# Moving the bias products and phi of a linear-attention stage off TensorE and VectorE

## What is computed

```python
x = x + 0.5 * ffn(layernorm(x))
x = x + attn(layernorm(x))
x = x + 0.5 * ffn(layernorm(x))

def attn(x):
    q = phi(split_heads(x @ Wq.T + bq))      # phi(z) = elu(z) + 1 = max(z, 0) + exp(min(z, 0))
    k = phi(split_heads(x @ Wk.T + bk))
    v = split_heads(x @ Wv.T + bv)
    kv_prefix = cumsum(k[..., :, None] * v[..., None, :], axis=rows)
    k_prefix = cumsum(k, axis=rows)
    out = (q . kv_prefix) / (q . k_prefix + 1e-6)
    return merge_heads(out) @ Wo.T + bo
```

## Time and profile before

| | |
|---|---|
| median of 3 runs | 388.18 us (387.33 to 390.04) |
| the profiled execution, own time | 387.34 us |
| its span in the profile | 385.6 us |
| PE, PEld busy | 312.6, 247.8 us |
| DVE, ACT, POOL busy | 228.4, 133.3, 241.6 us |
| mean granted TensorE clock | 0.91 |

### The profile page before, as it was taken

One profiled execution on the slowest core, in us unless ns is written; L12 is line 12 of the kernel. 1 busy time (PEld: TensorE's weight loads), 2 busy tenths in 40 slices (PEclk: granted clock), 3 DMA queues, 4 the chain that ended last, 5 costly groups with the idle time before them and its releaser, 6 DMA issues. The chain is left out here.

```text
span 385.6 us, 8340 instructions
## 1 busy us (share of the span) xinstructions
PE 312.6 (81%) x1964; PEld 247.8 (64%) x1970; DVE 228.4 (59%) x590; ACT 133.3 (35%) x375; POOL 241.6 (63%) x317
## 2 busy tenths in 40 slices
PE   2855699888888993899999999576798889989940
PEld 1832498887787871366677776333798788878820
DVE  5889364344333445979888889688244434333437
ACT  2205243332332335233455553333343223332322
POOL 5047567777777763564655556527677777777744
PEclk9997689999999997589999999655899999999995
DMA  7440466665555617000000000002476555555347
GB/s 210 139 122 2 109 153 192 159 164 163 135 155 162 164 48 218 2 0 0 15 14 14 12 9 20 24 7 60 126 194 166 154 159 152 152 155 156 111 146 202
DMA packets 35362, 41.88 MB, mean 109 GB/s; under 512 B 4808, under 2 KB 21840, under 8 KB 35344
## 3 DMA queue, kind: packets, MB, share of 16 engines
q1 hardware_dynamic: 30352, 31.44, 30.3%
q0 software_dynamic: 4992, 10.23, 8.8%
HBM read 33.39 MB, written 8.26 MB: 108 GB/s over the span
## 5 line engine op out<-in xcount | busy, mean ns | idle before, releaser
L401 POOL DMA_INDIRECT xg<-xn_rows,src_row x78 | 75.9, 973 | 33.3 <-issue 22.6
L408 POOL DMA_INDIRECT y_rows<-y_tile,dst_row x78 | 76.9, 985 | 24.0 <-issue 22.3
L1023 PE MATMUL banks<-xgT,w1b 128*128 128x128 f32 x624 | 89.1, 288 | 2.0 <-DMA w1b<-in_W1b 1.2
L768 DVE TENSOR_TENSOR h_pre<-banks,w1b 128x512 f32<-128x512 f32 x78 | 53.9, 691 | 58.4 <-PE banks L1023 57.0
L1032 PE MATMUL banks<-w,h_act 128*128 x624 | 87.1, 283 | 0.2
L1023 PEld LDWEIGHTS banks<-xgT,w1b 128*128 128x128 f32 x624 | 78.8, 198 | 4.9 <-DMA w1b<-in_W1b 1.4
L1032 PEld LDWEIGHTS banks<-w,h_act 128*128 128x128 f32 x624 | 75.5, 191 | 4.5 <-issue 0.8
L516 ACT COPY xgT<-banks 128x128 f32<-128x128 f32 x78 | 20.7, 265 | 125.7 <-PE banks L1042 125.7
L778 DVE COPY y_tile<-banks 128x128 f32<-128x128 f32 x78 | 22.7, 291 | 61.4 <-DMA y_rows<-y_tile,dst_row 55.5
L523 ACT ACTIVATE h_act<-h_pre 128x512 f32<-128x512 f32 x78 | 49.3, 632 | 5.8 <-DVE h_pre L768 5.8
L439 POOL TENSOR_TENSOR kv<-qk,vx 128x1024 f32<-128x1024 f32 x16 | 31.5, 1968 | 27.7 <-DVE qk L808 27.7
(11 more groups left out here) (182 smaller groups left out, 433.3 us busy)
## 6 DMA issues: line engine op xcount, KB each, us to landing
w1b<-in_W1b SPq DMA_DIRECT2D x78, 258.0 KB
y_back<-y_rows SPq DMA_DIRECT2D x16, 256.0 KB, 5.0
xg<-xn_rows,src_row POOLq DMA_INDIRECT x78
y_rows<-y_tile,dst_row POOLq DMA_INDIRECT x78
x<-in_L_attn_x SPq DMA_DIRECT2D x4, 256.0 KB, 3.8
xn_rows<-xn SPq DMA_DIRECT2D x4, 256.0 KB, 3.0
xn_rows<-xn_ring SPq DMA_DIRECT2D x16, 64.0 KB, 1.5
out<-x SPq DMA_DIRECT2D x4, 256.0 KB, 2.6
```

Source lines behind the costliest of these rows:

```text
L401: g.indirect_dma_start(out=xg[:, n % RING, :], out_offset=None, in_=xn_rows[f][:, :], in_offset=bass.IndirectOffsetOnAxis(ap=src_row[:, n: ...
L408: g.indirect_dma_start(out=y_rows[f][:, :], out_offset=bass.IndirectOffsetOnAxis(ap=dst_row[:, i:i + 1], axis=0), in_=y_tile[:, i % RING, ...
L768: v.tensor_tensor(h_pre[:, r, :].rearrange("p (c n) -> p c n", c=FC), h_bank(r).rearrange("p (c n) -> p c n", c=FC), w1b[:, r, DF:DF + FC] ...
L1023: last = mm(h_bank(q)[:, c * P:(c + 1) * P], w1b[:, q, c * P:(c + 1) * P], xgT[:, q, :], start=True, stop=True)
```

## The change

The attention's layer norm multiplies by `rstd` and adds `shift`. The new kernel adds 1 to the shift, so that each normed row sums to 128; it centres the weights (subtracts the mean over the input features) and adds bias / 128 to each of their rows. Three products on PE build this `w_fold` once. The host hands over the four weights turned and side by side, and the four biases as one row. The output bias is added to x by POOL for two tiles at a time (`add_bo`), and DVE's residual waits for it. The positive part of phi is a new ACT operation, `relu`, and the sum with `expo` is a new POOL operation at the head of `outer`.

```diff
@@ constants, loads
+            sp.dma_start(w_attn[:, :], Wa).then_inc(attn_in, 16)
+            sp.dma_start(bias[:, :], ba).then_inc(attn_in, 16)
             for t in range(NT):
                 sp.dma_start(b2_rep[t * E:(t + 1) * E, :], b2).then_inc(b2_in, 16)
-            for k, w in enumerate((Wq, Wk, Wv, Wo)):
-                sp.dma_start(w_raw[:, k, :], w).then_inc(attn_in, 16)
-            for k, b in enumerate((bq, bk, bv, bo)):
-                for a in range(2):
-                    sp.dma_start(bias[a:a + 1, k * P:(k + 1) * P], b.rearrange("(a d) -> a d", a=1)).then_inc(attn_in, 16)
...
+            g.memset(center[:, :], -1.0 / D).then_inc(const_step, 1)
+            pool.wait_ge(const_step, 15)
+            g.affine_select(out=center[:, :], in_=center[:, :], compare_op=ALU.not_equal, fill=1.0 - 1.0 / D, base=0,
+                            pattern=[[-1, P]], channel_multiplier=1).then_inc(center_ready, 1)
@@ POOL
             def outer(i, r):
+                pool.wait_ge(relu_sb, i + 1)
+                pool.wait_ge(exp_sb, i + 1)
+                g.tensor_tensor(qk[:, r, :], qk[:, r, :], expo[:, r, :], ALU.add).then_inc(phi_sb, 1)
                 pool.wait_ge(phi_sb, i + 1)
...
+            def add_bo(j):
+                pool.wait_ge(xa_sb, 2 * j + 2)
+                x2 = x[:, bass.ds(2 * j, 2), :]
+                g.tensor_tensor(x2, x2, w_fold[:, QD:].unsqueeze(1).to_broadcast([P, 2, P]), ALU.add).then_inc(bo_added, 1)
+
             outer(0, 0)
             reciprocal_root(1, CH, NT)
+            pool.wait_ge(fold_sb, 1)
+            add_bo(0)
             outer(1, 1)
             outer(2, 0)
+            add_bo(1)
             outer(3, 1)
             with pool.Fori(2, NT // 2) as j:
                 outer(2 * j, 0)
+                add_bo(j)
                 ln3_moments(j - 2)
                 outer(2 * j + 1, 1)
@@ ACT, pre()
+                at_least(act, prod_sb, i - 1)
+                s.activation(qk[:, r, :], qkv_bank[:, 0:2 * P], ACT.Relu).then_inc(relu_sb, 1)
                 if gate is not None:
                     turned_3(gate, r, xn_bank)
@@ DVE
                 v.scalar_tensor_tensor(out=shift[:, a:b], in0=mean[:, a:b], scalar=-1.0, in1=rstd[:, a:b],
-                                       op0=ALU.mult, op1=ALU.mult).then_inc(shift_ready, 1)
+                                       op0=ALU.mult, op1=ALU.mult).then_inc(shift_step, 1)
+                dve.wait_ge(shift_step, k + 1)
+                v.tensor_scalar(shift[:, a:b], shift[:, a:b], 1.0, None, ALU.add).then_inc(shift_ready, 1)
...
-                    dve.wait_ge(attn_in, 16 * 12)
-                    v.tensor_scalar(row_0[:, :], own_lane[0:2, :], 0.0, None, ALU.is_equal).then_inc(dve_step, 1)
...
-                    if f == 0 and t == NT - 3:
-                        phi(0, 0)
...
-            def residual(i):
+            def residual(i, pairs):
+                dve.wait_ge(bo_added, pairs)
                 dve.wait_ge(proj_ps, i + 1)
...
-                if phis:
-                    phi(i + 1, 1 - r)
@@ PE
-                pe.wait_ge(attn_in, 16 * 12)
-                for k in range(4):
-                    last = pe.transpose(banks[:, 7, k * P:(k + 1) * P], w_raw[:, k, :], ident[:, :])
-                last.then_inc(attn_w_ps, 1)
-                pe.wait_ge(attn_w_sb, 1)
+                pe.wait_ge(attn_in, 16 * 2)
+                pe.wait_ge(center_ready, 1)
+                mm(banks[:, 7, 0:QD], per_feature[:, :], bias[:, 0:QD], start=True, stop=False)
+                mm(banks[:, 7, 0:QD], center[:, :], w_attn[:, 0:QD], start=False, stop=True)
+                mm(banks[:, 7, QD:], tri[0:1, :], bias[:, QD:], start=True, stop=True).then_inc(fold_ps, 1)
+                pe.wait_ge(fold_sb, 1)
...
-                at_least(pe, phi_sb, i)
-                at_least(pe, exp_sb, i)
+                at_least(pe, relu_sb, i)
...
-                mm(qkv_bank, ones2[:, :], bias_2[:, 0:QD], start=True, stop=False)
                 pe.wait_ge(xaT_sb, i + 1)
-                mm(qkv_bank, xaT[:, r, :], wqkv, start=False, stop=True).then_inc(qkv_ps, 1)
+                mm(qkv_bank, xaT[:, r, :], wqkv, start=True, stop=True).then_inc(qkv_ps, 1)
...
-                mm(proj_bank, ones2[:, :], bias_2[:, QD:], start=True, stop=False)
-                mm(proj_bank, mT[:, r, :], w_attn[:, 3, :], start=False, stop=True).then_inc(proj_ps, 1)
+                mm(proj_bank, mT[:, r, :], w_attn[:, QD:], start=True, stop=True).then_inc(proj_ps, 1)
...
-            pe.wait_ge(bias_split, 1)
```

More of the change, by code:

```diff
@@ L35, in at_least, with macaron_kernel @@
     eng.wait_ge(sem, value)
-def macaron_kernel(nc, x_d, Wq, bq, Wk, bk, Wv, bv, Wo, bo, Wg, W1b, W2, b2, out_d):
+def macaron_kernel(nc, x_d, Wa, ba, Wg, W1b, W2, b2, out_d):
     T, D = x_d.shape[1], x_d.shape[2]
@@ L75, in macaron_kernel @@
         ones_bf = sb("ones_bf", [P, P], BF16)
-        ones2 = sb("ones2", [2, P], F32R)
+        per_feature = sb("per_feature", [1, P])
+        center = sb("center", [P, P])
         before = sb("before", [P, E, E])
@@ L92, in macaron_kernel @@
         wg = sb("wg", [P, E])
[L93 to L99, removed]
+        w_attn = sb("w_attn", [P, QD + P])
+        bias = sb("bias", [1, QD + P])
+        w_fold = sb("w_fold", [P, QD + P])
         x = sb("x", [P, NT, P])
@@ L207, in macaron_kernel @@
         const_step, consts, blank_ready = sem("const_step"), sem("consts"), sem("blank_ready")
-        attn_w_ps, attn_w_sb = sem("attn_w_ps"), sem("attn_w_sb")
+        center_ready, fold_ps, fold_sb, bo_added = map(sem, ("center_ready", "fold_ps", "fold_sb", "bo_added"))
+        shift_step = sem("shift_step")
         dve_step = sem("dve_step")
@@ L216, in macaron_kernel @@
             sem, ("att_var", "att_rstd", "ln3_root", "ln3_step", "ln3_ready"))
-        hi_ready, pair_ready, bias_split = sem("hi_ready"), sem("pair_ready"), sem("bias_split")
+        hi_ready, pair_ready = sem("hi_ready"), sem("pair_ready")
         y0_weighted, x_first, inter_ps = sem("y0_weighted"), sem("x_first"), sem("inter_ps")
@@ L227, in macaron_kernel @@
         xa_sb, xa_ps, xaT_sb, qkv_ps = map(sem, ("xa_sb", "xa_ps", "xaT_sb", "qkv_ps"))
-        neg_sb, exp_sb, v_sb, phi_sb = map(sem, ("neg_sb", "exp_sb", "v_sb", "phi_sb"))
+        neg_sb, exp_sb, v_sb, phi_sb, relu_sb = map(sem, ("neg_sb", "exp_sb", "v_sb", "phi_sb", "relu_sb"))
         qT_ps, qT_sb, kv_sb, prefix_ps = map(sem, ("qT_ps", "qT_sb", "kv_sb", "prefix_ps"))
@@ L346, in _ @@
             g.memset(ones_bf[:, :], 1.0).then_inc(consts, 1)
-            g.memset(ones2[:, :].bitcast(F32), 1.0).then_inc(consts, 1)
+            g.memset(per_feature[:, :], 1.0 / D).then_inc(consts, 1)
             g.affine_select(out=before[:, :, :], in_=before[:, :, :], compare_op=ALU.is_ge, fill=0.0, base=-1,
@@ L377, in _ @@
             g.memset(eps[:, :], LN_EPS).then_inc(const_step, 1)
-            pool.wait_ge(const_step, 14)
+            g.memset(center[:, :], -1.0 / D).then_inc(const_step, 1)
+            pool.wait_ge(const_step, 15)
+            g.affine_select(out=center[:, :], in_=center[:, :], compare_op=ALU.not_equal, fill=1.0 - 1.0 / D, base=0,
+                            pattern=[[-1, P]], channel_multiplier=1).then_inc(center_ready, 1)
             g.memset(vx[:, :, :, :], 1.0).then_inc(consts, 1)
@@ L492, in ffn @@
                 if f == 0:
-                    act.wait_ge(attn_w_ps, 1)
-                    s.copy(w_attn[:, :, :].rearrange("p k n -> p (k n)"), banks[:, 7, :]).then_inc(attn_w_sb, 1)
+                    act.wait_ge(fold_ps, 1)
+                    s.copy(w_fold[:, :], banks[:, 7, :]).then_inc(fold_sb, 1)
                 act.wait_ge(lo_ready, f + 1)
@@ L784, in experts @@
                 output(0, 0)
-                if f == 0:
-                    dve.wait_ge(attn_in, 16 * 12)
-                    v.tensor_scalar(row_0[:, :], own_lane[0:2, :], 0.0, None, ALU.is_equal).then_inc(dve_step, 1)
[L789 to L794, removed]
                 with dve.Fori(1, NS // RING) as j:
@@ L800, in experts @@
                 output(NS // RING - 1, RING - 1)
[L802 to L809, removed]
             def combine(f):
@@ L863, in _, with attend @@
             combine(0)
-            def attend(i, r):
+            def attend(i, r, pairs=0):
                 first = isinstance(i, int) and i == 0
@@ L881, in attend @@
                 if not first:
-                    residual(i - 1)
+                    residual(i - 1, pairs)
                 dve.wait_ge(nd_sb, i + 1)
@@ L905, in moments, with attn @@
                            x[:, bass.ds(i, 1), :].rearrange("p a d -> p (a d)")).then_inc(stats_ready, 1)
-            def attn(i, r, phis=True):
-                if phis:
-                    phi(i + 1, 1 - r)
-                attend(i, r)
+            def attn(i, r, pairs):
+                attend(i, r, pairs)
                 if isinstance(i, int) and i == 0:
@@ L914, in _ @@
             for i in range(2):
```

(17 more changed lines are left out.)

## The result

The changed kernel takes 393.29 us as a median (391.08 to 394.58, 4 runs), against 387.75 us (386.64 to 390.04, 4 runs) for the kernel before beside it: a ratio of 1.016, interval 1.012 to 1.020. The profiled execution took 394.58 us, of which the span is 392.7, against 387.34 and 385.6.

What follows compares the result with a forecast made beforehand. PE was taken to bound attention, DVE close behind, POOL with room. 387.34 + 3.7 (attention: lead-in holds less loop gains) - 0.3 (start) = 390.7, as a median 391.6 us; range 386.0 to 396.0.

Steps and rivals of the forecast that it cites:

- PE's 0.61 us a tile: Attention loop: two PE operations per tile go, 0.36 and 0.25 us, 9.8 us in all if nothing else is late.
- The cycle: Attention loop: chain through POOL, ACT and PE takes 9.79 us for two tiles against 9.94, gaining 0.9 us in all.
- The shared port: DVE operations with both inputs in SBUF stand still while POOL runs one; `merged` now can, in the lead-in.
- (3): Lead-in: DVE's variance operations meet the first outer product, end near 164.5, so the root ends near 166.8.
- (4): Lead-in: behind pair 0's bias and phi(1), 0.72 us each, `outer(1)` starts at 168.3 instead of 166.54, +1.7.
- (5): Lead-in: second shift meets `outer(2)`, the +1 meets pair 1's bias; `prod` of tile 1 near 173.7, not 171.25, +2.4.
- (6): Lead-in: `merged` of tile 1 meets `outer(3)`, up to 2 us; PE's turn of it and that round wait.
- a low clock longer: Rival, lead-in: PE idles more, its clock may rise later, 2 us more, 393.6; inside the forecast's range, no separate chance.
- Start: Before attention: later b2 copies and L382, PE ready 0.4 us earlier for the counts; -0.3 us taken in all.
- PE as the bound: Rival, attention loop: PE is the bound and gets its 0.61 us a tile, 378.4 us; chance 0.06.
- the holds miss: Rival: the lead-in loses little and the loop runs at 4.9 us, 386.4 us; chance 0.24.
- `merged` held in every pair: Rival, attention loop: DVE waits up to 1.9 us for POOL, about +1.2 in each of six pairs, 399; chance 0.12.

Runs made afterwards that it cites:

- fold alone: The changed kernel with phi back on DVE (no relu on ACT, no sum on POOL): 387.49 us against 386.85 for the kernel before, ratio 1.002.
- PSUM: The changed kernel with the denominator and its reciprocal in PSUM: 389.39 us, ratio 1.009 to the kernel before.
- late bias: The changed kernel with POOL's output-bias sum moved behind the pair's second outer product: 387.49 us, ratio 1.005 to the kernel before.
- `mT` in the changed kernel: The changed kernel with ACT's copy `mT` put ahead of `norm_3` and nothing else: ratio 1.006 to the kernel before, on the third chip.
- the changed kernel's second: The changed kernel run again, unaltered, on the third chip: ratio 1.008 to the kernel before.
- the first eight experiments: The follow-up runs on the first two chips, four on each, where the kernel before takes 386.85 and 385.47 us.

## Why the prediction was right or wrong

The time (391.6, measured 393.3) and its range held. The side of the 1% mark did not: "within 1%" had more weight than "slower", and it was slower.

**PE's 0.61 us a tile can't be used: right.** PE 9.02 of 10. POOL is at 8.12, not "over 9": its pair costs 2 x (0.73 + 1.97) + 0.73 + 2.81 = 8.9 us, but of 10.1 and not of 9.8.

**The cycle: right chain, one link read from the wrong row.** By the rows after, from the end of the moments (211.17): 0.35 to `norm_3`, 0.40, 0.30, 0.43, 0.85, 1.32 to the end of exp, 0.15 to phi's sum, 0.88 to the outer product, 1.92, 0.68 and 2.81 for the moments, 10.09 in all; predicted 9.79. Of the 0.30, the hand-over from POOL's last moment to ACT is all: I took 0.04 for it, which in the earlier trace rows is what PE to ACT takes. The trace of before had the right one, 205.00 to 205.35, and I did not read it. The link after the change, and below it the one before:
```profile
210.98 0.19 POOL L462 TENSOR_TENSOR shift<-halves,rstd 128x2 f32 x1 [0.17 <-POOL rstd L460]
211.52 0.49 ACT L566 ACTIVATE xn_ring<-x,shift,rstd 128x128 f32 x1 [1.85 <-POOL shift L462]
```
```profile
205.35 0.49 ACT L555 ACTIVATE xn_ring<-x,shift,rstd 128x128 f32 x1 [0.29 <-POOL shift L461]
```
The other links differ by at most 0.11, and these cancel. The prediction gave the six pairs a gain of 0.9 us. The loop lost 0.9 from tile 5 to 13 and another 0.7 up to tile 15, where PE waits 1.09 us for the last outer product (243.84). That is 2.5 us of attention's 6.3, and the term that was mis-sized: it makes up nearly all of the difference between +3.7 and +6.3. Moving the bias sum out of the cycle gave 0.68 a pair of the 0.72 that the cycle has for it, so POOL's moments and what stands ahead of them are in the cycle; that is shown, and not only fitted. The link from the moments to `mT` is shown less well: cut, it gave about 0.3 a pair and not 0.6 to 1.0, so another chain must be nearly as long there.

**The shared port: shown, with the half that no row had shown.** `merged` was always 0.37 us and is now held in single tiles, in the lead-in above all (0.49, 0.80 and 1.91 us); with the bias sum late it is held in the loop too, in three of its tiles for 0.87 to 0.94 us; with the reciprocal in PSUM none is, and attention is 3.4 us shorter in the profile. By the Trainium skill (SBUF — State Buffer, "Who interferes with whom") scalar forms from SBUF to SBUF, those with one input, can be held too. The rows agree: 1.82, 1.78, 0.91 and 0.65 us for operations of 4 to 16 columns, and 1.22 for the denominator in fold alone.

**Lead-in steps.** (2) `outer(0)` at 161.8: 162.12. (3) root ends 166.8: 166.98, though of the variance operations only L668 was held, which has one input. (4) `outer(1)` at 168.3: 168.44. (5) `prod` of tile 1 at 173.7: 174.70, but for another reason. The +1 was held as taken (1.78 us, by `outer(2)`), yet DVE then idled 1.53 us for PE's prefix product, which took 2.93 instead of 1.46 us at the low clock. (6) `merged` of tile 1 meets `outer(3)`, up to 2 us: it didn't. At 178.51 it lost about 0.4 us beside phi's sum (178.33). The long hold fell on tile 2, behind `outer(4)`, a meeting that no step had. Tile 5 late by 4.5 to 5: 4.8. So the total is right in part by luck: neither the low clock at tile 1, nor that hold, nor the fall of the clock at 188 behind it was in the sum. As a rival of +2 us "a low clock longer" was named and left out of the forecast. It belonged in: behind the same wait of 1.71 us the low clock came in four of the five profiles that have it (the changed kernel's first, PSUM, late bias, `mT` in the changed kernel), and not in the fifth (the changed kernel's second).

**Start: right in number, and that may be luck.** The b2 copies came 0.6 us later and L382 with them, DVE was held by it for 3.61 us again, and the feed-forward's end came 0.3 earlier, as taken. But attention's first residual, up to which seven of the first eight experiments run the changed kernel's code, lies anywhere from 146.2 to 149.8 us in these seven. A step of 0.3 can't be read from two profiles.

**Behind attention: missed.** 1.1 us in the second feed-forward stage. The code there is the same in both kernels, and the stretch from attention's last residual to the end of the span takes 139.6 to 141.9 us in the profiles of the first eight experiments; 140.0 before and 141.1 after both lie within that. So the 1.1 us need not come from the change.

**The rivals.** PE as the bound and "the holds miss" fell by the rows above. `merged` held in every pair doesn't happen: 0.36 to 0.37 us in the loop, 1.91 in one tile ahead of that. Fold alone at 1.002, and not the 381 to 384 expected, shows that I still counted a gain on PE as a gain in time: its waits for the outer product and for `mT`, and the clock, took it.

**Open.** Which execution shows a low clock, and where, differs: the changed kernel's four runs go from 391.08 us at a mean clock of 0.931 to 394.58 at 0.907. So the profiled one is the longest of them, and a part of its 6.3 us is its own. The kernel before has a low clock in the lead-in too, up to 166, where the changed one is at full clock from 164: the prefix product of tile 0 takes 2.77 us before and 1.56 after, that of tile 1 takes 1.47 before and 2.93 after. What the two gain and lose by it cancels in part, in a way that I can't take apart. And the size of the loss is open: 1.016 (1.012 to 1.020) as first measured, 1.008 (1.004 to 1.013) on the third chip.

## What to carry to other kernels

Moving work off two full engines pays only if the wait that follows the move is shorter than what it frees: lay out one period of every cycle through the engine that receives it, with each hand-over read between that very pair of engines, before counting busy time. Put what nobody waits for soon (here the bias sum, and `norm_3`) behind what the full engine waits for: with the bias sum late the fold went from 1.002 to 0.995, and with `mT` first as well (and the denominator in PSUM, whose own share can't be told) to 0.987, the last on another chip. Where DVE and POOL work beside each other, give a short DVE operation a PSUM operand, and count a PE stop of 2 us with the slower products behind it.

## What the runs showed of the hardware

Short stops of PE in the lead-in and the loop of attention, where it is otherwise nearly full, can be followed by the lower clock: stops of 1.91 to 2.61 us (seven, in as many profiles) each were, with prefix products of 2.26 to 2.93 us instead of 1.46; those of 1.71 us in four of five; one of 1.55 and one of 1.78 us were not. The length of one stop doesn't decide it alone: in fold alone the clock fell at 206 behind none over 0.81 us (PE busy 0.84, 0.41 and 0.78 us in the three from 203 to 206). It stayed low for 3 to 7 us. A DVE operation on 4 to 16 columns took up to 1.82 us beside POOL operations on SBUF, and 0.16 to 0.33 (the denominator in the loop) when it wasn't held. Two dependent POOL operations stand 0.08 to 0.18 us apart, POOL to ACT 0.35. On the third chip the kernel before took 36 us longer (423.7 against 387.75); for the changed kernel, 15 of its 31 us more of span lie ahead of attention and attention is no longer (99.9 against 101.6). Why is open.
